# Both tiles of a sequence in one matmul per recurrence level, with an order of pieces for each engine

## The reference

```
L0_attn: proj = x @ W_in -> z, x_raw, B, C, dt_raw, lambda_raw, theta_raw
         dt = clip(softplus(dt_raw + dt_bias), 1e-4, 0.5);  lam = sigmoid(lambda_raw)
         B, C = rope(rms_norm(.) * bias, cumsum(mean(dt) * theta_raw))
         y = ssd(x * lam, B) + ssd(shift(x) * (1 - lam) * alpha, shift(B))   # alpha = exp(A * dt)
         ssd: y[l] = sum over s <= l of (C[l] . B[s]) * exp(cs[l] - cs[s]) * dt[s] * x[s],
              64 heads of 8 columns, cs = cumsum(dt * A) per head
         out = (rms_norm(y) * silu(z)) @ W_out
L0_ffn:  (silu(x @ Wg.T) * (x @ Wu.T)) @ Wd.T, hidden 704, integer weights with scales
L1_attn: qkv = rms(x) @ w_qkv.T;  w = exp(rms(k));  y = sigmoid(rms(q)) * cumsum(w * v) / cumsum(w)
         x + (u * silu(g)) @ w_out.T,  [u, g] = y @ w_swiglu.T, 1024 wide
L1_ffn:  16 experts, the top 4 of each token, hidden 448
```

## Time and profile before

| | |
|---|---|
| median of three runs | 2329.75 us |
| the profiled execution: time / span | 2336.15 us / 2334.3 us |
| TensorE clock granted, mean | 0.944 of full speed |
| first block, up to the first instructions of the second | about 0 to 1580 us |
| distance between rounds | 92.2 us (the sum at line 1167 starts at 91.4 us in the first round and at 1474.9 us, 15 rounds later) |
| one round (921.6 to 1013.8 us): PE / DVE / POOL / ACT busy | 83.2 / 66.4 / 46.6 / 32.1 us |
| expert layers and combination | 1580 to 2334.3 us |

### The profile page before, as it was taken

The page is one execution under the profiler, slowest core; times in us unless marked ns, Lnnn a source line. Parts: engine busy times, 40 slices in busy tenths (PEclk is TensorE's granted clock), DMA queues, the critical chain, the costliest instruction groups (busy, mean ns, idle before and its releaser), DMA issues. The chain is left out here.

```text
span 2334.3 us, 35408 instructions
## 1 busy us (share of the span) xinstructions
PE 1989.1 (85%) x9748; PEld 1376.3 (59%) x9749; DVE 1374.6 (59%) x2699; ACT 725.1 (31%) x1473; POOL 1137.6 (49%) x903
## 2 busy tenths in 40 slices
PE   4599989989999899899899998754799999999990
PEld 2366656656656566566566665542466666666660
DVE  4686776776766867867767678321344444444445
ACT  2224333243333343332433333211222223223223
POOL 2352554554554535545545455212355555555554
PEclk7799999999999999999999999876899999999995
DMA  6111101111111111011111111007733333333347
GB/s 232 36 43 45 54 29 55 40 38 58 44 38 50 43 39 57 28 54 39 38 58 44 38 50 32 22 14 207 231 58 61 59 59 59 59 59 59 59 56 225
DMA packets 141648, 149.94 MB, mean 64 GB/s; under 512 B 36321, under 2 KB 131745, under 8 KB 141217
## 3 DMA queue, kind: packets, MB, share of 16 engines
q1 hardware_dynamic: 105504, 107.13, 15.1%
q0 software_dynamic: 31744, 38.04, 10.2%
q10 hardware_dynamic: 4352, 4.20, 0.5%
HBM read 89.96 MB, written 59.34 MB: 64 GB/s over the span
## 5 line engine op out<-in xcount | busy, mean ns | idle before, releaser
L1005 POOL TENSOR_TENSOR y<-y,v 128x1024 f32<-128x1024 f32 (+1 forms) x128 | 332.4, 2597 | 144.9 <-DVE v L1153 139.4
L1495 PE MATMUL pu<-w_ug,xh 128*128 x1728 | 362.6, 358 | 20.5 <-issue 11.8
L1634 POOL DMA_INDIRECT sums_dram<-yo,meta_in x144 | 227.8, 1582 | 255.8 <-DVE yo L1604 241.2
L1588 DVE TENSOR_TENSOR gate_hid<-pu,gate_hid 128x448 f32<-128x448 f32 x144 | 90.0, 625 | 362.1 <-ACT gate_hid L1556 362.1
L739 PE MATMUL pb<-x1T,w_sw 128*128 128x256 f32 x1024 | 259.1, 407 | 12.5 <-ACT x1T L848 11.0
L1495 PEld LDWEIGHTS pu<-w_ug,xh 128*128 128x128 bf16 x1728 | 169.3, 99 | 170.1 <-issue 46.6
L739 PEld LDWEIGHTS pb<-x1T,w_sw 128*128 128x128 f32 x1024 | 207.9, 205 | 76.9 <-issue 24.4
L1556 ACT ACTIVATE gate_hid<-pu 128x448 f32<-128x448 f32 x144 | 78.2, 543 | 456.8 <-PE pu L1495 425.5
L634 PE MATMUL pa<-u,masked 128*128 128x512 f32 x448 | 208.8, 601 | 10.8 <-DVE u L1143 6.5
L1521 PE MATMUL py<-w_dn,hh 112*128 x1728 | 215.5, 275 | 1.1 <-DVE yo L1604 1.1
L1143 DVE TENSOR_TENSOR u<-xg,decay 128x1024 f32<-128x1024 f32 (+1 forms) x128 | 179.0, 1428 | 50.5 <-ACT decay L821 50.5
(11 more groups left out here) (228 smaller groups left out, 3346.6 us busy)
## 6 DMA issues: line engine op xcount, KB each, us to landing
w_stage<-in_w_ug SPq DMA_DIRECT2D x64, 224.0 KB, 2.8
split_ug<-w_parts SPq DMA_DIRECT2D x64, 224.0 KB, 2.4
w_ug<-split_ug SPq DMA_DIRECT2D x16, 896.0 KB, 11.3
rows<-sums_dram SPq DMA_DIRECT2D x32, 256.0 KB, 5.3
w_stage<-in_w_dn SPq DMA_DIRECT2D x32, 224.0 KB, 2.9
split_dn<-w_parts SPq DMA_DIRECT2D x32, 224.0 KB, 2.8
w_dn<-split_dn SPq DMA_DIRECT2D x16, 448.0 KB, 12.5
xT<-in_xT SPq DMA_DIRECT2D x16, 256.0 KB, 2.7
```

The lines of the kernel that those rows point to most:

```text
L1005: nc.gpsimd.tensor_tensor(y[:, first:NT, :], y[:, first:NT, :], v[:, k % 2, first:NT, :], ALU.add).then_inc(y_added.sem, 1)
L1495: last = mm(pu[:, 2 * b + w, 0:EH], xh[:, b, xp, c, :], w_ug[:, bass.ds(e, 1), wp, c, w * EH:(w + 1) * EH], start=n == 0, stop=n == 3 * DC ...
L1634: nc.gpsimd.indirect_dma_start(out=sums_dram[m % 2], out_offset=bass.IndirectOffsetOnAxis(ap=meta[:, m, 0:1], axis=0), in_=yo[:, m % 2, :] ...
```

## The change

- **One matmul per level.** The host hands over the second tile of each sequence, and takes it back, in reverse order of tokens. A level then moves data from left to right halves in tile 0 and from right to left halves in tile 1, so the two use different rows and different quadrants of one 128x128 matrix. `xgs[k]` holds in each row the `xg` of the tile that sends from that row. The seven levels now run on 128x512 instead of 128x1024, each with one 512-column matmul instead of two. They are taken in the order 0, 6, 1, 5, 2, 4, 3.
- **`xgs` is made by DMAs**, SBUF to SBUF, from `xg`: 12 for the first four levels and 32 for the other three, all issued by SP, 44 a sequence.
- **Masks and scales by predicated copies on DVE**: two of 128x896 for `masked`, two of 128x448 and a product of 128x896 for the decays. POOL's masks are gone.
- **Sums of y on DVE**: POOL's eight additions become 14 instructions of 128x512 (`AY`), each of which adds the rows of one tile, and one addition.
- **An order for each engine**, so that the same piece may stand at another place, or in another round, on each; a `+` or `-` moves a piece to the next or the former sequence. F is split: F3 (z) stays, and the rest becomes G, which runs for the next sequence beside the levels.
- ACT computes `alpha` (128x128) and `from_first` (128x448) besides; the PE matmuls of A2 become six of 64 or 32 columns instead of four.

```diff
-ORDER = (["F1", "D8", "F2", "B1T", "F4.0", "C7", "B1.0", "C7L", "B1.1", "WH.0", "F4.1", "B1.2", "F4.2", "B1.3", "WL.0", "B1.4"]
...
+LEVELS = (0, 6, 1, 5, 2, 4, 3)
+EARLY = 4
+ORDER = {
+    "SP": ("N0 A2 WL.5- C7 WL.0 WL.1 WL.2 WL.3 WL.4 A0+"),
+    "POOL": ("A6- A2 A2L D8+ B2 B3 G1+ A5 B6"),
...
+            def select_halves(s):
+                sp.wait_ge(xg_ready.sem, xg_ready.at(s))
...
+                for n, k in enumerate(LEVELS):
+                    q = 2 ** k
+                    by_row = q <= P // (2 * q)
+                    for t in range(NT):
+                        if by_row:
+                            rows = [slice(t * q + i, P, 2 * q) for i in range(q)]
+                        else:
+                            rows = [slice(i * 2 * q + t * q, i * 2 * q + (t + 1) * q) for i in range(P // (2 * q))]
+                        for r in rows:
+                            sp.dma_start(xgs[r, k, :], xg[r, t, :]).then_inc(xgs_in[n >= EARLY].sem, 16)
...
             def a4(s, n):                                                   # PE
+                if n == 0:
                     pe.wait_ge(decay_ready.sem, decay_ready.at(s))
-                    pe.wait_ge(masked_ready.sem, masked_ready.at(s, NT))
+                    pe.wait_ge(masked_ready.sem, masked_ready.at(s))
                     pe.wait_ge(cb_copied.sem, cb_copied.at(s))
...
-                    for t in range(NT):
-                        last = mm(pa[:, 2 * (k % 2) + t, :], masked[:, t, k, :], u[:, k % US, t, :],
-                                  start=True, stop=True)
+                weights = masked[:, LEVELS[n], :] if n < LV else cb_cross[:, :]
+                mm(pa[:, n % 2, :], weights, u[:, n % US, :], start=True, stop=True).then_inc(level_done.sem, 1)
...
             def a2_late(s):                                                 # ACT
                 act.wait_ge(decay_sums.sem, decay_sums.at(s))
                 act_f(decay[:, :, :, :].rearrange("p k t h -> p (k t h)"),
-                      pa[:, 0:2, :].rearrange("p b n -> p (b n)"), ACT.Exp).then_inc(decay_ready.sem, 1)
+                      pa[:, 0:2, :].rearrange("p b n -> p (b n)"), ACT.Exp)
+                act_f(from_first[:, :, :], pa[:, 0:2, :].rearrange("p b (k t h) -> p (b k) t h", t=NT, h=H)[:, 0:LV, 0, :],
+                      ACT.Exp).then_inc(decay_ready.sem, 1)
...
-            def mask(s, k0, k1):                                            # POOL
-                for t in range(NT):
-                    nc.gpsimd.tensor_tensor(masked[:, t, k0:k1, :], spread(cb_all[:, t, :], 1, k1 - k0),
-                                            const[:, MASK0 + k0:MASK0 + k1, :], ALU.mult
-                                            ).then_inc(masked_ready.sem, 1)
...
+            def a3_late(s):                                                 # DVE
+                dve.wait_ge(cb_ready.sem, cb_ready.at(s))
+                carrier.take()
+                for t in range(NT):
+                    vec.copy_predicated(masked[:, :, :], halves[:, t, :, :], spread(pa[:, 2, t * P:(t + 1) * P], 1, LV)
+                                        ).then_inc(masked_ready.sem, 1)
...
+            def decayed(s, n):                                              # DVE
+                if n == 0:
+                    dve.wait_ge(xgs_in[0].sem, xgs_in[0].at(s))
+                elif n == EARLY:
+                    dve.wait_ge(xgs_in[1].sem, xgs_in[1].at(s))
...
+                vec.tensor_tensor(by_head(u[:, n % US, :]), by_head(src), spread(by, 2, HD), ALU.mult
+                                  ).then_inc(u_ready.sem, 1)
...
+            def a4_sum(s, n):                                               # DVE
...
+                for t in range(NT):
+                    o = SM_HALF + t * LV + k
+                    vec.scalar_tensor_tensor(y[:, t, :], v[:, n % 2, :], small[:, o:o + 1], y[:, t, :], ALU.mult, ALU.add
+                                             ).then_inc(y_added.sem, 1)
```

More of the change, by code:

```diff
@@ L682, in b1 @@
                 last.then_inc(ffn_projected.sem, 1)
-            def b2(s):
-                if later(s):
-                    pe.wait_ge(meta_ready.sem, meta_ready.before(s))
-                pe.wait_ge(ffn_h.sem, ffn_h.at(s, FJ - 1))
-                for t in range(NT):
-                    for j in range(FJ):
-                        if t == 0 and j == FJ - 1:
-                            pe.wait_ge(ffn_h.sem, ffn_h.at(s))
-                        rows = min(P, FH - j * P)
-                        last = mm(pb[:, 3, t * D:(t + 1) * D], hT[0:rows, j, t * P:(t + 1) * P], w_down[0:rows, j, :],
-                                  start=j == 0, stop=j == FJ - 1)
-                last.then_inc(ffn_out.sem, 1)
@@ L698, in b3_first, with b2 @@
-            def b3_first(s):
-                transposes(x2n, x2n_ready, x2_transposed, s)
-            def b3(s):
-                pe.wait_ge(x2T_ready.sem, x2T_ready.at(s))
-                for t in range(NT):
-                    for c in range(DC):
-                        last = mm(pb[:, 1 + t, :], x1T[:, c, t * P:(t + 1) * P], w_qkv[:, c, 0:2 * D],
-                                  start=c == 0, stop=c == DC - 1)
-                    last.then_inc(qk_projected.sem, 1)
+            def b2(s, t):
+                if t == 0:
+                    if later(s):
+                        pe.wait_ge(meta_ready.sem, meta_ready.before(s))
+                    pe.wait_ge(ffn_h.sem, ffn_h.at(s, FJ - 1))
+                for j in range(FJ):
+                    if t == 0 and j == FJ - 1:
+                        pe.wait_ge(ffn_h.sem, ffn_h.at(s))
+                    rows = min(P, FH - j * P)
+                    last = mm(pb[:, 3, t * D:(t + 1) * D], hT[0:rows, j, t * P:(t + 1) * P], w_down[0:rows, j, :],
+                              start=j == 0, stop=j == FJ - 1)
+                if t == NT - 1:
+                    last.then_inc(ffn_out.sem, 1)
@@ new lines, in b3_first, with b3, b3_v @@
+            def b3_first(s):
+                transposes(x2n, x2n_ready, rows_transposed, s)
+            def b3(s, t):
+                if t == 0:
+                    pe.wait_ge(columns_ready.sem, columns_ready.at(s, 2))
+                for c in range(DC):
+                    last = mm(pb[:, 1 + t, :], x1T[:, c, t * P:(t + 1) * P], w_qkv[:, c, 0:2 * D],
+                              start=c == 0, stop=c == DC - 1)
+                last.then_inc(qk_projected.sem, 1)
+            def b3_v(s):
@@ L1096, in f4 @@
                 last.then_inc(steps_ready.sem, 1)
+                cg.end()
             def a2(s):
-                ca.go_on(s)
+                ca.start(s)
                 dve.wait_ge(shifted.sem, shifted.at(s))
@@ L1235, in b4 @@
             def b4(s, part):
+                cb_.go_on(s)
                 if part == 1:
@@ L1792, in host_arrays @@
         "empty": empty_slots(x.shape[0]),
-        "matrices": constant_matrices(), "small": small_constants(tile_count(x.shape[0])),
+        "halves": halves_of_levels(), "right": right_half(), "matrices": constant_matrices(), "small": small_constants(tile_count(x.shape[0])),
     }
@@ L1808 @@
     r = _run(nc, [arrays], core_ids=[0])
-    return r.results[0]["out"].reshape(shape)
+    return second_tile_reversed(r.results[0]["out"]).reshape(shape)
```

409 lines of the change are left out of this document (231 added, 178 removed), and 12 rows, old and new, of the table ORDER.

## The result

The changed kernel takes 2445.0 us (median of 4 runs, 2443.4 to 2446.4), the kernel before 2331.2 us beside it (4 runs, 2326.4 to 2338.2): ratio 1.0486, 95% interval 1.0457 to 1.0514. It is slower by almost 5%. I had predicted 2290 us, with 2185 to 2375 for 8 times in 10, so the time lies outside the range, on the side to which I had given 0.24. The order of events in a round is the one predicted. The price of a copy on SP is not.

What follows compares the result with a forecast made beforehand. PE was the bound: round 92.2 - 6.1 - 6.8, taken as 79, + 10.1 + 1.6 - 1.7 = 89.0 us; 2336 - 48 + 18 - 9 = 2297, predicted 2290 us, 8-in-10 range 2185 to 2375.

Steps and rivals of the forecast that it cites:

- the side to which I had given 0.24: Whole kernel: the chance of 0.24 that the changed kernel is slower than the one before.
- 44 copies at 0.47 us: SP's queue: the copies making xgs take 20.5 us a round, priced from 17 back-to-back DMAs.
- The rival at 0.6 us: SP's copies: at 0.6 us each they take 26.4 us, round 94.9, kernel slower at 2386 us; chance 0.17.
- The rest of the chain: Behind the copies: SP's queue 3.6 us, landing 2.8, ACT's and DVE's parts, masks 2.2; first level 10.1 us late.
- the late level: First level on PE: waits for DVE's masks, queued behind weight piece 2 and the copies; 10.1 us late a round.
- PE's savings: PE, each round: merged levels save 6.1 us, fewer waits and less slow clock in the new order 6.8.
- if nothing new waits: Round without new waits: 92.2 us less both savings on PE, giving 79.3 us, taken as 79.
- slow clock at 1.6: PE behind the wait at the first level: matmuls at the lower clock level add 1.6 us a round.
- hT behind the first u: First feed-forward layer: hT pieces stand behind the first u on DVE, out at 15.6 us; PE waits 2.7 us.
- first rival: Copies at 0.33 us don't hold levels up: PE waits 3 us, too short for lower clock; 2196 us, chance 0.2.
- DVE: DVE stays near 66 us a round, below PE's 77, and is no bound in the sum.
- Outside the rounds: First round 18 us longer; end 9 us shorter, because the last routing no longer waits for earlier routes' stores.

Runs made afterwards that it cites:

- experiment 5: Separate small kernel, run once: SP issues groups of 16 DMAs back to back; 64 rows inside SBUF took 0.635 us each, 8-row loads from DRAM 0.36.
- experiment 6: Second separate kernel, run once, other DMA sizes: inside SBUF 16 rows 0.62 us each; 128 rows of 512 bytes with one side in DRAM 0.47.
- experiment 3: Changed kernel with 14 copies of 64 rows a sequence instead of 44, same bytes, output not the reference's: 2185.6 us, ratio 0.935 to the kernel before.
- experiment 7: Changed kernel with eight copies of 16 rows split into sixteen of 8, 52 copies instead of 44, same bytes: 2514.9 us, ratio 1.074 to the kernel before.
- experiment 4: experiment 1 with the first and fifth u also moved later on DVE: 2140.8 us, ratio 0.916 to the kernel before, round 79.4 us.
- experiment 8: Changed kernel with only DVE's low parts of weight pieces 1 and 2 moved behind the level additions, ACT's parts unmoved: 2487.6 us, ratio 1.062.
- experiment 10: experiment 4 with 52 copies instead of 44: 2236.2 us, ratio 0.957 to the kernel before, round 85.7 us.
- experiment 12: Changed kernel with SP's stores of weight pieces 5 and 0 and loads of pieces 1 and 2 ahead of the 44 copies: 2430.1 us, ratio 1.041.
- experiment 1: Changed kernel with weight pieces 1 and 2 on ACT and DVE moved behind the first levels, ACT's piece 3 slightly later: 2237.6 us, ratio 0.957.

## Why the prediction was wrong

- **The failed term: 44 copies at 0.47 us.** They took 27.4 us, 0.62 each, instead of 20.5. The text had the right limit ("from 0.53 us a copy, the kernel is slower") and even the reason ("the source and the target are both in SBUF"), but it took the value from the nearest-looking row, 17 stores to DRAM. Experiments 5 and 6 show that those are another price list, experiments 3 and 7 that the round follows the copies, not their bytes. By itself the term is worth 6.9 us a round, 15 x 6.9 = 103 of the 155 us between forecast and result. The rival at 0.6 us gave 2386 us, 59 too low.
- **The rest of the chain** was short by small terms in one direction. From the start of a round (the end of PE's w_out, 997.3 us here) the first level was to begin after 37.7 us and began after 47.5. 6.9 of the 9.8 us are the copies. They start 1.2 us later, since the load of x_row, which stands ahead of xT, waits for L1310. That takes 2.48 us for its two beside POOL, where two of its kind take 0.74 (995.88 us), as in the earlier trace rows (L1315); the queue behind them takes 4.7 us instead of 3.6, the landing and its parts 0.4 more, the masks 2.6 instead of 2.2.
- **From the first level to the round's end** 51.3 us had been forecast and 51.3 were measured. That they agree so closely is partly luck: in experiment 4 this stretch takes 50.2 us where the forecast had 51.4 without the late level, and the wait ahead of it adds 1.2 us (slow matmuls, less a wait saved) where the forecast had -0.1.
- **PE's savings** held: 79.3 us if nothing new waits, 79.4 in experiment 4. In the changed kernel PE is busy for 78.3 us, with a clock of 0.91. That is 3.1 above experiment 4, where the forecast had put slow clock at 1.6.
- **hT behind the first u:** 2.7 us forecast, 5.4 measured, again for the copies' price and start (u done at 18.1 instead of 15.6 us), with the first four matmuls slow behind it (2.08 and 1.62 us for two, against 1.03). The text had no slow clock here. Its first rival called a wait of 3 us too short for that; in experiment 3 a wait of 3.16 us is followed by pairs of matmuls at 1.34, 1.91 and 1.70 us, so it isn't.
- **DVE** as forecast: 65.4 us (66), additions at 0.75 us (0.7), predicated copies of 896 columns at 1.15 (1.1). It is no bound. L1428 at 0.64 us (0.61) shows that POOL's additions no longer stand beside it.
- **Outside the rounds:** +21.3 us for the first (18), -11.4 at the end (-9).
- **On the Trainium skill** (DMA: Bandwidth & Descriptors, Why a DMA increments its semaphore by 16 and not by 1): by its rule copies of 8 rows use 8 engines and the issuing sequencer writes the rest of the 16 itself. No trace here shows these writes; the times are these. Inside SBUF 8 rows cost 0.67 us where 16 cost 0.62, and 0.61 when the 8 are spread over every 16th partition. With a side in DRAM 8 rows cost only 0.33 to 0.36. In the large kernel the copies of 8 rows are no dearer (52 copies: 31.97 us, 0.61 each). I had read the rule as speaking for more than 0.47 us; the price is there for 64 rows too, so the rule isn't its cause.

The chance of 0.17 for the slower side by the copy's price was too small. The bounds ran from 0.33 to 0.80 us, the threshold lay at 0.53, close above my value, and of the rows only the store at 0.60 us in the earlier trace rows, which I named and set aside, spoke for 0.62.

## What to carry to other kernels

A burst of small DMAs is priced by their number, about 0.62 us each inside SBUF on one queue (8 to 64 rows of 2 KB here), and the work queued behind the burst pays for it: look for what each engine has in line behind the first transfer that follows. Before believing a gain of a new order, measure the one unit price that is multiplied by 44, by itself, for that very source, target and size. Where a piece of work may be late, move all of its stages on all engines behind what is urgent; moving one stage alone made it worse.

## What the runs showed of the hardware beside this

- SP takes 0.61 to 0.68 us for each copy inside SBUF of 8 to 64 rows of 2 KB, and no less for the smallest; transfers of 8 rows with a side in DRAM take 0.33 to 0.36. Why is open.
- In experiments 8, 10 and 12 the addition behind w_down starts 2.8 to 5.0 us (mostly 4.2 to 4.8) after PE's timeline has it end, in 14, 14 and 13 of 16 rounds, with ACT released at the same moment in experiment 10. It begins while SP issues copies and POOL its last scatters. The first round, which has copies and no scatters, and the last, which has scatters and no copies, never show it (0.05 us at most). Yet both overlap at the same times in experiments 1 and 4, which don't show it either (0.13 us). Moving the scatters removed it once. What holds the signals back is open.
